# A two-layer block on one core: a re-timed column pipeline, one of four gated expert tiles moved to ScalarE and GpSimd, biases folded into weights

## The reference

```python
# 1: attention among the 16 images at each of the 4096 positions, 8 heads of 16 channels
zn = norm(x) * ln_w + ln_b
q, k, v = zn @ Wq, zn @ Wk, zn @ Wv;  g = sigmoid(zn @ Wg + bg)
x = x + (softmax(q k^T / 4) v * g) @ Wo + bo
# 2: mixture of 8 experts, the two likeliest of each token
t = norm(x)
x = x + sum over the two of p_e * (t @ expert_w[e] + expert_b[e])   # p from softmax(t @ router_w + router_b)
# 3: gated moving average along the first image axis (64 rows)
e = norm(x) @ W_exp.T + b_exp;  prim, gate = split(e)
x = x + (prim * sigmoid(ema(gate))) @ W_con.T + b_con
# 4: each of 32 experts picks 8 of the 4096 tokens of an image, softmax over tokens
n = norm(x);  logits = n @ gate_w.T + gate_b
x = x + scatter(mlp_e(pooled picked tokens) * weights)
```

## Time and profile before

| | |
|---|---|
| median of 3 runs | 2711.42 us (2711.4 to 2712.73) |
| the profiled execution's own time | 2704.94 us |
| its span | 2703.1 us |
| TensorE busy | 2383.0 us (88%) |
| VectorE busy | 2245.5 us (83%) |
| GpSimd busy | 2107.5 us (78%) |
| ScalarE busy | 1657.3 us (61%) |
| granted TensorE clock, mean | 0.937 |

### The profile page before, as it was taken

One profiled execution on the slowest core, in us unless ns is written; L12 is line 12 of the kernel. 1 busy time (PEld: TensorE's weight loads), 2 busy tenths in 40 slices (PEclk: granted clock), 3 DMA queues, 4 the chain that ended last, 5 costly groups with the idle time before them and its releaser, 6 DMA issues. The chain is left out here.

```text
span 2703.1 us, 127455 instructions
## 1 busy us (share of the span) xinstructions
PE 2383.0 (88%) x45291; PEld 1715.2 (63%) x45291; DVE 2245.5 (83%) x8757; ACT 1657.3 (61%) x3077; POOL 2107.5 (78%) x3098
## 2 busy tenths in 40 slices
PE   4999999999999999999999999999999999997368
PEld 3666666666666666666666666666666666664258
DVE  3688898898888988889888898888988889886626
ACT  3556666666666666666666666666676666663330
POOL 3677788888888888888888888888888888885310
PEclk9888899999999999999999999999999999996579
DMA  1001111111111111111111111111111111111579
GB/s 22 9 18 22 21 22 20 22 20 21 22 19 23 20 21 22 20 23 20 21 22 20 22 20 21 21 20 23 19 21 22 20 23 20 21 21 16 175 280 373
DMA packets 263185, 107.28 MB, mean 40 GB/s; under 512 B 251284, under 2 KB 253882, under 8 KB 259003
## 3 DMA queue, kind: packets, MB, share of 16 engines
q1 hardware_dynamic: 260831, 101.54, 16.0%
q10 hardware_dynamic: 2268, 4.57, 0.5%
HBM read 55.56 MB, written 50.33 MB: 39 GB/s over the span
## 5 line engine op out<-in xcount | busy, mean ns | idle before, releaser
L516 ACT ACTIVATE kT<-shared,b_k,quarter 128x512 f32<-128x512 f32 x512 | 364.3, 789 | 0.0
L835 DVE TENSOR_TENSOR yg<-shared,gates 128x512 f32<-128x512 f32 x512 | 344.7, 685 | 22.9 <-PE shared L646 22.5
L932 DVE TENSOR_REDUCE mixed<-yg 128x256 f32<-128x2048 f32 x128 | 285.5, 2231 | 0.3
L460 POOL TENSOR_TENSOR probs<-weights,own_den 128x1024 f32<-128x1024 f32 x128 | 247.3, 1932 | 17.0
L645 PE MATMUL shared<-w_expert_hi,tT 128*128 128x512 f32 x512 | 260.5, 509 | 0.0
L653 PE MATMUL shared<-w_o,ogT 128*128 128x64 f32 x2048 | 255.2, 279 | 4.6 <-DVE ogT L975 4.4
L653 PEld LDWEIGHTS shared<-w_o,ogT 128*128 128x128 f32 x2048 | 245.3, 196 | 15.5 <-DVE ogT L975 9.5
L701 PE MATMUL shared<-ident,split_conv 128*128 128x128 f32 x512 | 100.0, 328 | 146.6 <-POOL split_conv L427 146.6
L546 ACT COPY lT<-shared 64x512 f32<-64x512 f32 x128 | 74.1, 579 | 222.5 <-PE shared L674 222.5
L646 PE MATMUL shared<-w_expert_lo,tT 128*128 128x512 f32 x512 | 204.5, 399 | 0.0
L731 PEld LDWEIGHTS o_bank<-probsT,v_sb 32*32 32x32 f32 x16384 | 165.4, 104 | 59.9 <-issue 54.8
(11 more groups left out here) (200 smaller groups left out, 7139.0 us busy)
## 6 DMA issues: line engine op xcount, KB each, us to landing
x_in<-in_x SPq DMA_DIRECT2D x1024, 16.0 KB, 1.7
x_scratch<-x SPq DMA_DIRECT2D x1024, 16.0 KB, 1.5
normalized_x_scratch<-norm_pick SPq DMA_DIRECT2D x1024, 16.0 KB, 1.4
xa<-normalized_x_scratch SPq DMA_DIRECT2D x8, 1024.0 KB, 8.1
xc<-normalized_x_scratch SPq DMA_DIRECT2D x8, 1024.0 KB, 12.5
out_x<-xc SPq DMA_DIRECT2D x16, 512.0 KB, 5.3
xc<-x_scratch SPq DMA_DIRECT2D x4, 1024.0 KB, 8.4
xb<-x_scratch SPq DMA_DIRECT2D x4, 1024.0 KB, 17.0
```

Of the source, the lines that this page charges most:

```text
L460: g.tensor_tensor(probs[:], weights[:].unsqueeze(2).broadcast_to([P, 32, 2, 16]), own_den[:].unsqueeze(3).broadcast_to([P, 32, 2, 16]), AL ...
L516: ins = s.activation(kT[:, h, :], bk("k"), ACT.Identity, bias=b_k[:, h:h + 1], scale=quarter[:, h:h + 1])
L835: v.tensor_tensor(yg[:, t], bk(y).rearrange("p (d e) -> p d e", e=NE), gates[:, t, :].unsqueeze(1).broadcast_to([P, D, NE]), ALU.mult).the ...
L932: v.tensor_reduce(mixed[:], yg[:], AX.X, ALU.add).then_inc(s_mixed, 1)
```

## The change

Most of it is a new table of lags, a new order on every engine and other banks. Beside it, work moves and goes:

- Biases of q, k, v, of the experts and of the router are folded into the weights: the normalized rows keep 63 of their 64 channels (`LAST`), the 64th is a constant 1, and `to_rows` (a small matrix product at start-up) rewrites the weights for it. The bias products in front of `y0` to `y3` and `v` go. `bo` and `b_con` are added by a bf16 product of 256 columns in front of `att_out` and `scan_out`; instead of GpSimd's `xbo` and `x2bc`, ScalarE copies (`xkeep`, `x2keep`).
- The means of `W_exp` and `gate_w` are taken out of these weights, so `sub_conv` and `sub_pick` go. In the tail, three small ScalarE operations take the mean out of `pooled`.
- `gated` moves from VectorE to GpSimd, as one instruction on a masked, doubled tanh that ScalarE lays out (`ema1`, two instructions in every second slot).
- Tile 3 of the experts: ScalarE copies it out of PSUM (`y3A`), GpSimd multiplies it by the gates (`yg3`); the other three stay on VectorE.
- `gates` and `lgm` move from VectorE to GpSimd, `lg` and `top2` from VectorE to ScalarE.

```diff
 STAGES = {
-    4: "r1_ffn sub_ffn pow_ffn mul_ffn lo_ffn rnd_ffn tT att_out ffn_t route x1 st_ffn ag_ffn lg max lgm",
-    5: "x2 r1_conv pow_conv lge y0 y3 y2 y1 top2 mrep sel gden grec gates yg0 yg3 yg2 yg1 mixed st_conv "
-       "ag_conv",
-    6: "sub_conv mul_conv lo_conv x2bc rnd_conv cT exA conv_t expand scan",
-    7: "ema",
-    8: "x3st r1_pick scan_out gated x3 st_pick ag_pick",
+    4: "r1_ffn att_out og x1 st_ffn ag_ffn",
+    5: "sub_ffn pow_ffn mul_ffn lo_ffn lgm rnd_ffn tT lg top2 y3A lge ffn_t route y3 y0 y2 max mrep sel "
+       "gden grec",
+    6: "gates yg3 x2 r1_conv pow_conv y1 yg2 yg0 yg1 mixed st_conv ag_conv",
+    7: "mul_conv lo_conv rnd_conv cT exA conv_t expand",
+    8: "x2keep ema ema1 scan",
+    9: "x3st gated scan_out x3",
+    10: "r1_pick st_pick ag_pick",
...
-PEELED = 7
+PEELED = 8
...
+                    if runs(i, q, "yg3"):
+                        pool.wait_ge(drained["y3"], at(i, q, "yg3"))
+                        pool.wait_ge(s_gates, at(i, q, "yg3"))
+                        wait(pool, s_mixed, at(i, q, "yg3", 1))
+                        g.tensor_tensor(yg[:, 3], y3[:], gates[:, 3, :].unsqueeze(1).broadcast_to([P, D, NE]), ALU.mult).then_inc(s_yg3, 1)
...
+                        g.tensor_tensor(gated[z][:].rearrange("p a (h n) -> p a h n", h=2), ema_own[:, half],
+                                        prim[:, half, :].unsqueeze(2).broadcast_to([P, A // 2, 2, 8]), ALU.mult).then_inc(s_gated, 1)
...
-                            ins = s.activation(kT[:, h, :], bk("k"), ACT.Identity, bias=b_k[:, h:h + 1],
-                                               scale=quarter[:, h:h + 1])
+                            ins = s.mul(kT[:, h, :], bk("k"), quarter[:, h:h + 1])
...
+                    if par(q, "ema1") == 1 and runs(i, q, "ema1"):
+                        act.wait_ge(s_tanh, column(i, q, "ema1") + 1)
+                        wait(act, s_gated, at(i, q, "ema1", 2))
+                        for h in range(2):
+                            ins = s.activation(ema_own[:, :, h, :], ema_t[:], ACT.Identity, bias=half_of[:, h:h + 1], scale=half_of[:, h:h + 1])
+                        ins.then_inc(s_emat, 1)
...
+                    if runs(i, q, "y3A"):
+                        act.wait_ge(filled["y3"], at(i, q, "y3A"))
+                        wait(act, s_yg3, at(i, q, "y3A", 1))
+                        s.copy(y3[:].rearrange("p d e -> p (d e)"), bk("y3")).then_inc(drained["y3"], 1)
...
-                        t_.matmul(bk(y), ones3[:], bias3[:], start=True, stop=False)
-                        t_.matmul(bk(y), tT[z][:, tile(t)], w_expert_hi[:], start=False, stop=False)
+                        t_.matmul(bk(y), tT[z][:, tile(t)], w_expert_hi[:], start=True, stop=False)
...
+                        t_.matmul(bk("att_out")[:, 0:QT * D], ones3[:], b3[:, 0, :], start=True, stop=False)
```

More of the change, by code:

```diff
@@ L44 @@
-    7: "ema",
-    8: "x3st r1_pick scan_out gated x3 st_pick ag_pick",
-    9: "sub_pick pow_pick mul_pick",
-    10: "n3st lT pick_t pick",
-    11: "picks",
+    0: "xload",
+    1: "st_att",
+    2: "r1_att sub_att pow_att mul_att lo_att rnd_att xkeep zT qA km0 km1 att_t q k ag_att",
+    3: "own probs gateA vA exp gp1 v gate scores values smax sub ssum rec probsT",
+    4: "r1_ffn att_out og x1 st_ffn ag_ffn",
+    5: "sub_ffn pow_ffn mul_ffn lo_ffn lgm rnd_ffn tT lg top2 y3A lge ffn_t route y3 y0 y2 max mrep sel "
+       "gden grec",
@@ new lines, in step @@
+                        ins.then_inc(filled["ffn_t"], 1)
+                    if runs(i, q, "att_out"):
+                        bank_free(pe, i, q, "att_out")
+                        pe.wait_ge(drained["values"], at(i, q, "att_out"))
+                        t_.matmul(bk("att_out")[:, 0:QT * D], ones3[:], b3[:, 0, :], start=True, stop=False)
+                        for t in range(QT):
+                            for h in range(2):
+                                ins = t_.matmul(bk("att_out")[:, t * D:(t + 1) * D], ogT[:, h, tile(t)], w_o2[:, h, :],
+                                                start=False, stop=(t == QT - 1 and h == 1))
+                        ins.then_inc(filled["att_out"], 1)
@@ L844, in step @@
-                    if runs(i, q, "gated"):
-                        z = par(q, "gated")
-                        dve.wait_ge(s_emat, column(i, q, "gated") + 1)
-                        wait(dve, filled["scan_out"], at(i, q, "gated", 2))
-                        half = slice(z * 32, (z + 1) * 32)
-                        for h in range(2):
-                            rows = slice(h * D, (h + 1) * D)
-                            ins = v.scalar_tensor_tensor(gated[z][rows, :, h * 8:(h + 1) * 8],
-                                                         ema_t[rows, half, :], 1.0, prim[rows, half, :], ALU.add, ALU.mult)
-                        ins.then_inc(s_gated, 1)
@@ L928, in step @@
-                    if runs(i, q, "mixed"):
-                        for t in range(QT):
-                            dve.wait_ge(drained[f"y{t}"], at(i, q, "mixed"))
-                        wait(dve, s_x2, at(i, q, "mixed", 1))
-                        v.tensor_reduce(mixed[:], yg[:], AX.X, ALU.add).then_inc(s_mixed, 1)
                     if runs(i, q, "st_pick"):
@@ new lines, in step @@
+                    if runs(i, q, "ssum"):
+                        dve.wait_ge(s_exp, at(i, q, "ssum"))
+                        wait(dve, s_own, at(i, q, "ssum", 1))
+                        v.tensor_reduce(ssum[:], weights[:], AX.X, ALU.add).then_inc(s_sums, 1)
+                    if runs(i, q, "max"):
+                        wait_apart(dve, (drained["route"], at(i, q, "max")), (s_diff, at(i, q, "max", 1)), (s_top2, at(i, q, "max", 1)))
+                        for t in range(QT):
+                            ins = v.max(top8[:, t, :], lg[:, t, :])
+                        ins.then_inc(s_top, 1)
```

823 lines of the change are left out of this document (420 added, 403 removed).

## The result

The changed kernel takes 2584.63 us (median of 4 runs, 2580.65 to 2614.94) against 2711.41: ratio 0.955, 95% interval 0.949 to 0.962. It is faster by 127 us, where 151 were forecast; the time lies in the range and nearest to the likeliest case. The terms of the sum did not all hold. Two more executions took 2587.96 and 2620.29 us, the second at the lowest clock of all (0.871).

A forecast was written before the change was run, and what follows sets the result against it. It took one round, TensorE, VectorE, GpSimd, TensorE, closed within a slot of 18.77 us, as the bound. New slot 17.04 + 0.2 + 0.1 = 17.34 us; 2704.9 - 156 + 5 = 2554, median 6.5 above: 2560 us, range 2475 to 2690.

The forecast's parts named there:

- the likeliest case: Whole kernel: the forecast itself, a slot of 17.34 us and 2560 us in all, chance 0.50.
- The round is cut: Column loop: GpSimd no longer needs `conv_t` of the same slot to begin `rstd_conv`; slot falls to fullest engine or next round.
- GpSimd is the fullest: Column loop: GpSimd's own work, 17.04 us a slot, sets the new slot; TensorE at most 16.3.
- The unseen prices: GpSimd's added instructions, priced from other rows: `yg3` and `gated` 1.31 us each, `gates` and `lgm` 0.24 each.
- Scan, 0.4 in every second slot: VectorE's scan beside GpSimd: charges GpSimd 0.4 us in every second slot, 0.2 a slot.
- The bound of 1.2: Upper bound of the scan's charge to GpSimd: the whole of a scan, 1.2 us, in every second slot.
- Small waits, 0.1: Column loop: 0.1 us a slot added for small waits at hand-overs to GpSimd.
- Every hand-over back to GpSimd closes: Column loop: other engines' results reach GpSimd in time, with 0 to 1 us to spare.
- The ends, +5: Outside the even stretch: later first `mixed` +13.6, start-up +3, tail +1, 19 surrounding slots -13; together +5 us.
- cheaper products: Rival, GpSimd: `yg3` and `gated` take 1.05 us and the scan costs nothing; slot 16.6, 2479 us; chance 0.19.
- shared path costs more: Rival, GpSimd beside VectorE: both products 1.66 us, scan stops GpSimd 1.2 us; slot 18.4, 2680 us; chance 0.20.
- A new round through ScalarE: Rival: `lgm`, ScalarE's `lge`, `sel`, `ag_conv`, `rstd_conv` make GpSimd wait every slot; slot 19.5, 2800 us; chance 0.05.

The follow-up runs named there:

- experiment 6: Changed kernel with the fourth gated tile multiplied by VectorE instead of GpSimd, from ScalarE's copy, which stays: 2493.38 us, ratio 0.918.
- experiment 1: Changed kernel with `sel` and `gden` moved behind `ag_conv`, `x3` and `ag_ffn` on VectorE: 2542.28 us, ratio 0.938.
- experiment 9 (b): Kernel of experiment 8 with only a wait for `gates` put ahead of the scan on VectorE: 2437.61 us.
- experiment 8: Changed kernel with `sel` behind `ag_ffn`, scan ahead of `yg2`, `rstd_pick`'s power ahead of `norm_conv`, and the fourth tile's product on VectorE: 2443.20 us, ratio 0.897.
- experiment 4: Kernel before the change, with only `ag_conv` moved ahead of `scan` and `lg` on VectorE: 2660.79 us, ratio 0.983.
- experiment 5: Changed kernel with three constant 512-column products added on TensorE ahead of its wait for `split_ffn`: 2574.28 us.

## Why the prediction was right, and where it was not

- *The round is cut*: right. TensorE's waits for `split_conv` fell from 146.6 us in 119 times to 1.2 in 2, and opening that round alone, in the kernel before, gave 52 us. The rest came from the order as a whole; no run splits it further.
- *GpSimd is the fullest*: right, by experiment 6. Its work is the undisturbed slot without a scan less its wait, 17.26 - 0.50 = 16.76 us, forecast 17.04. The unseen prices (`yg3`, `gated` 1.31, small products 0.24) measured 1.28, 1.27 and 0.24.
- *Scan, 0.4 in every second slot*: mis-sized. It cost 18.19 - 17.26 = 0.93, so 0.46 a slot instead of 0.2. The guess took over what `gated` had cost (0.22 and 0.16 us, in the mean), but a hold lasts to the end of the instruction that came first, and the scan is longer and had just begun. The bound of 1.2 was nearer.
- *Small waits, 0.1*: the step that failed. "Every hand-over back to GpSimd closes" took `sel` at its short length; beside `probs` it took 1.59, and 0.50 a slot came of it; `rstd_conv`'s wait of under 0.3, the prediction's own sign of being right, did not come.
- The corrections make up 17.34 - 0.28 + 0.26 + 0.40 = 17.72, against 17.73 measured. This is bookkeeping and no test, since all three are taken from the same two slots; the tests are experiment 1, where 0.42 of the 0.50 goes, and the rows of the holds.
- *The clock*: not in the sum. The 18.77 of before held a quarter of a microsecond for it; the new slot was given none, and had 0.6 in the profiled run. In the median run, 30 us shorter, it is by an estimate 30/127 = 0.24 less, if all of the difference is the clock.
- *The ends, +5*: measured -14 (-18 and +4), although the first `mixed` is one slot further on. The first slots wait less for each other; this was not taken apart.
- The errors offset each other in part: the loop of the profiled run gave 76 us, where 156 and 13 were forecast. A forecast within 25 us is better than its steps.
- *A slip*: in "cheaper products" GpSimd needs 17.04 - 2 x 0.26 = 16.52, not 16.3 to 16.4; the slot of 16.6 and the 2479 go by the right figure.
- *Rivals*: "shared path costs more" had the mechanism right for the scan (0.9 of its 1.2) and wrong for the two products. The Trainium skill (GPSIMD Engine Reference, Key points) states the contention for instructions with two SBUF inputs; the traces agree (`mv_conv` free, `sel` held beside the same `probs`) and add how long. "A new round through ScalarE" named `sel` and `rstd_conv`, and there the wait is, but for another reason: ScalarE's `lge` was in time, waiting itself for GpSimd's `lgm`.

The version that beats both the kernel before and the changed one by most is that of experiment 9 (b), 2437.61 us, ratio 0.896 (0.890 to 0.903), with that of experiment 8 not to be told from it.

## What to carry to other kernels

Before giving GpSimd more elementwise work, lay its instructions beside VectorE's two-operand instructions from SBUF: the later one waits for the other whatever its size (a power of GpSimd already under way was the one exception), and what stands behind it in the queue waits too. The profile counts the hold as busy time, so it stands in no list of waits; look for rows that are longer than their equals. A short instruction that takes a microsecond and ends with the other engine's long one is the sign; moving it behind VectorE's instructions that aren't held cost nothing here and gave 42 us. Once GpSimd is relieved, a stall taken off it may be worth nothing: look who waits next. And look at rows from stretches at the full clock and below it apart: the engines shift against each other, and the scan caught another instruction in each.

## What the runs showed of the hardware

- `sel` (32 columns, two SBUF operands): 0.16 us clear of `probs` (experiment 1), 0.27 when begun 0.22 us before its end, 1.59 when begun 0.4 us into it. `mv_conv`, one operand: 0.36 us beside `probs`. `og`, one operand from PSUM and one from SBUF: its usual 0.68 wholly beside `probs` (59 times in experiment 4).
- GpSimd's instructions begun under a scan: `norm_ffn` 1.52 for 0.61, `gates` 1.15 for 0.24, the power 1.77 and 1.89 for 1.00, and with a single operand `rstd_pick` from `mv_pick` 1.04 for 0.19 (experiment 4). No instruction that GpSimd began under a scan was spared in any of the traces, save in the scan's last quarter of a microsecond. A power begun 0.1 to 0.9 us before the scan took its usual 1.01, and the scan its usual 1.21; beside a product over 252 columns already under way the scan took 1.39.
- TensorE's clock fell to 0.50 in a stretch in which TensorE is recorded as busy throughout (experiment 5).
